# ScalarE makes the normalised nodes of a four-layer graph network's first and last layer, one activation per unit

## What is computed

```python
h = jnp.maximum(_layernorm(x, axis=-1), 0.0)
x = x + _L0_gnn_ref(h, adj, W, b)      # norm = (degree + 1e-6)^-0.5
                                       # elu(adj @ (h @ W * norm) * norm + b)
h = jnp.maximum(_layernorm(x, axis=-1), 0.0)
x = x + _L1_gnn_ref(h, adj, att_w, att_b)   # hyperbolic attention, log and exp maps
h = jnp.maximum(_layernorm(x, axis=-1), 0.0)
x = x + _L2_gnn_ref(h, adj, ...)       # message of every edge: layernorm, gelu; weighted sum
h = jnp.maximum(_layernorm(x, axis=-1), 0.0)
x = x + _L3_gnn_ref(h, adj, ...)       # four dense layers over row- and column-normed adj, tanh
```

## Time and profile before

| | us |
|---|---|
| median of three runs | 4520.15 (4515.0 to 4526.37) |
| the profiled execution, device time | 4512.91 |
| its span, first to last instruction | 4511.1 |
| mean granted TensorE clock | 0.911 of full speed |

### The profile page before, as it was taken

One profiled execution on the slowest core, in us unless ns is written; L12 is line 12 of the kernel. 1 busy time (PEld: TensorE's weight loads), 2 busy tenths in 40 slices (PEclk: granted clock), 3 DMA queues, 4 the chain that ended last, 5 costly groups with the idle time before them and its releaser, 6 DMA issues.

```text
span 4511.1 us, 101660 instructions
## 1 busy us (share of the span) xinstructions
PE 3669.4 (81%) x30593; PEld 3151.2 (70%) x31028; DVE 3454.1 (77%) x12581; ACT 2807.4 (62%) x6445; POOL 2195.7 (49%) x2282
## 2 busy tenths in 40 slices
PE   3484988879888788888878888788878878888898
PEld 2373867768677677767768677676867767676787
DVE  4788987879778687877868778786887868787750
ACT  3474856748566584765748576574856748485553
POOL 1282925528264371835628173471826528183540
PEclk7695999989899899998999899999999999999999
DMA  2000000010000101000010000001000010000000
GB/s 73 24 1 24 0 10 29 1 39 0 13 27 1 39 0 31 8 10 29 1 39 1 19 20 10 29 1 39 0 16 23 1 39 0 10 14 1 15 1 19
DMA packets 95516, 74.04 MB, mean 16 GB/s; under 512 B 7504, under 2 KB 95184, under 8 KB 95184
## 3 DMA queue, kind: packets, MB, share of 16 engines
q1 hardware_dynamic: 95184, 70.09, 5.1%
HBM read 61.68 MB, written 8.39 MB: 16 GB/s over the span
## 4 chain that ended last, share of the span: by engine, by line
PE 38%; DVE 25%; ACT 17%; issue 13%; DVEq 2%; ACTq 1%; POOL 1%; DMA 0%; SPq 0%; POOLq 0%
DVE v_z L1071 6%; PE n_bank_c L1551 6%; PE n_bank_d L1565 5%; PE n_bank_d L1568 5%; PE n_bank_d L1569 4%; PE n_bank_b L1454 4%; DVE v_pstats L1079 4%; ACT v_diag L739 4%; PE n_bank_c L1454 3%; DVE v_onehot L1061 2%; ACT v_msg L734 2%; ACT v_rows L776 1%; PE n_bank_a L1666 1%; PE n_bank_d L1465 1%; DVE v_normed L1113 1%
## 5 line engine op out<-in xcount | busy, mean ns | idle before, releaser
L516 POOL TENSOR_TENSOR v_z<-v_z,all_bc_L_gnn_be 128x512 f32<-128x512 f32 x620 | 814.3, 1314 | 86.4 <-DVE v_z L1071 86.4
L532 POOL TENSOR_TENSOR v_prstd<-v_pvar,all_neg_half 128x4 f32<-128x4 f32 x620 | 665.8, 1074 | 132.1 <-DVE v_pvar L1088 127.6
L1465 PE MATMUL n_bank_d<-v_diag,v_msg 128*128 128x128 f32 x4960 | 618.3, 278 | 24.6 <-ACT v_diag L739 24.6
L1454 PEld LDWEIGHTS n_bank_b<-v_parts,v_onehot 128*128 128x128 bf16 x8208 | 495.3, 101 | 145.4 <-ACT n_bank_b L680 101.1
L1465 PEld LDWEIGHTS n_bank_d<-v_diag,v_msg 128*128 128x128 f32 x4960 | 576.9, 192 | 27.6 <-ACT v_diag L739 27.6
L1454 PE MATMUL n_bank_b<-v_parts,v_onehot 128*128 128x128 bf16 x8208 | 535.0, 224 | 70.5 <-ACT n_bank_b L680 62.6
L739 ACT ACTIVATE v_diag<-all_ident,v_value 128x128 f32<-128x128 f32 x1860 | 572.7, 387 | 0.0
L1454 PEld LDWEIGHTS n_bank_c<-v_parts,v_onehot 128*128 128x128 bf16 x7440 | 444.2, 100 | 149.2 <-ACT n_bank_c L680 109.4
L1454 PE MATMUL n_bank_c<-v_parts,v_onehot 128*128 128x128 bf16 x7440 | 479.7, 222 | 84.2 <-ACT n_bank_c L680 81.4
L1551 PE MATMUL n_bank_c<-all_l_wsd,v_fT 128*128 128x256 f32 x1792 | 453.7, 395 | 29.4 <-ACT v_adjT L665 26.1
L675 ACT ACTIVATE v_fT<-n_bank_d,all_l_c 128x256 f32<-128x256 f32 x256 | 121.4, 475 | 530.1 <-PE n_bank_d L1569 530.1
(11 more groups left out here) (280 smaller groups left out, 7569.8 us busy)
## 6 DMA issues: line engine op xcount, KB each, us to landing
v_adj_l<-in_adj SPq DMA_DIRECT2D x128, 256.0 KB, 3.6
v_adj_x<-in_adj SPq DMA_DIRECT2D x64, 256.0 KB, 3.6
v_ring<-in_x SPq DMA_DIRECT2D x16, 512.0 KB, 5.4
out_x<-v_xout SPq DMA_DIRECT2D x64, 128.0 KB, 1.8
w_wu<-in_L_gnn_wu SPq DMA_DIRECT2D x4, 192.0 KB, 2.6
all_W<-in_L_gnn_W SPq DMA_DIRECT2D x2, 128.0 KB, 4.4
w_raw<-in_L_gnn_ws SPq DMA_DIRECT2D x1, 192.0 KB, 3.0
w_raw<-in_L_gnn_wd SPq DMA_DIRECT2D x1, 192.0 KB, 3.2
```

Source lines behind the costliest of these rows:

```text
L516: nc.gpsimd.tensor_tensor(z[par][:, units], z[par][:, units], wide(bc["L2_gnn_be1"])[:, units], ALU.add).then_inc(sem["z_ready"], 1)
L532: nc.gpsimd.tensor_tensor(prstd[:, units], pvar[:, units], minus_half[:, units], ALU.pow).then_inc(sem["prstd_ready"], 1)
L1454: ins = nc.tensor.matmul(ps_m[par][:, u], onehot[:, par, k, u * P:(u + 1) * P], parts[:, b * NB + k, t], start=False, stop=False, skip_gro ...
L1465: ins = nc.tensor.matmul(ps_agg[:, u // NB, (u % NB) * P:(u % NB + 1) * P], msg[par][:, u], diag[par][:, u], start=False, stop=False, skip ...
```

## The change

VectorE no longer makes the two sets of nodes. It makes, for all eight units at once, a scale and a bias per node (128x8 each), and ScalarE makes the nodes in one activation per unit, relu(scale * x + bias). For layer 0 the scale is rstd * norm and the bias is -mean * rstd * norm (norm is positive, so it may go inside the relu); for layer 3 they are rstd3 and -mean * rstd3. On VectorE layer0_scales stands where layer0_scaled stood, layer0_normed goes, and last_bias stands where last_features stood. On ScalarE layer0_nodes stands behind the table load L840 and before the first copy of layer 0's turned adjacency, last_nodes behind the eight Exp and before keep_sd(2). There are two new semaphores, scale0_ready and bias3_ready; hn_ready and h3_ready now come from ScalarE. In the prologue layer0_nodes(0) stands between the sign counts and the copies of the turned adjacency.

```diff
+            def layer0_nodes(z_):
+                act.wait_ge(sem["scale0_ready"], z_ + 1)
+                act.sem_inc(keep["held"], 1)
+                first = act.snap((z_ % RING) * GB)
+                xg = ring[:, bass.ds(first, GB)].rearrange("p b k d -> p (b k) d")
+                for u in range(UNITS):
+                    ins = nc.scalar.activation(hn[:, u], xg[:, u], ACT.Relu, bias=bias0[:, u:u + 1], scale=scale0[:, u:u + 1])
+                    if u % NB == NB - 1:
+                        ins.then_inc(sem["hn_ready"], 1)
+
+            def last_nodes(g):
+                act.wait_ge(sem["bias3_ready"], g + 1)
+                act.sem_inc(keep["held"], 1)
+                first = act.snap((g % RING) * GB)
+                xg = ring[:, bass.ds(first, GB)].rearrange("p b k d -> p (b k) d")
+                flat = h3[:].rearrange("p b k d -> p (b k) d")
+                for u in range(UNITS):
+                    ins = nc.scalar.activation(flat[:, u], xg[:, u], ACT.Relu, bias=bias3[:, u:u + 1], scale=rstd3[:, u:u + 1])
+                ins.then_inc(sem["h3_ready"], 1)
...
                     act.preload_act_table_set(EXP_TABLES)
+                if l0:
+                    layer0_nodes(z_)
+                if l1:
                     if l0:
                         act.wait_ge(sem["gated"], a * GB + GB)
...
                         nc.scalar.activation(total[:, b], total[:, b], ACT.Exp, scale=-0.5).then_inc(sem["coef_ready"], 1)
+                if u:
+                    last_nodes(g)
                 if l3:
                     keep_sd(t, 2, 0)
...
                 count_signs(0, u)
+            layer0_nodes(0)
             for b in range(GB):
                 layer0_keep_adjT(0, b)
...
-            def layer0_normed(z_):
+            def layer0_scales(z_):
                 dve.wait_ge(sem["rstd0_ready"], z_ + 1)
-                xg = nodes(z_)
-                for u in range(UNITS):
-                    v.tensor_scalar(normed[:, u], xg[:, u], mv0[:, u, 0:1], rstd[:, u:u + 1], ALU.subtract, ALU.mult)
+                dve.wait_ge(sem["norm_ready"], z_ + 1)
+                v.tensor_tensor(scale0[:], rstd[:], norm[:], ALU.mult)
                 dve.drain()
-
-            def layer0_scaled(z_):
-                dve.wait_ge(sem["norm_ready"], z_ + 1)
-                for b in range(GB):
-                    for u in range(b * NB, (b + 1) * NB):
-                        ins = v.tensor_scalar(hn[:, u], normed[:, u], 0.0, norm[:, u:u + 1], ALU.max, ALU.mult)
-                    ins.then_inc(sem["hn_ready"], 1)
+                v.scalar_tensor_tensor(bias0[:], mv0[:, :, 0], -1.0, scale0[:], ALU.mult, ALU.mult)\
+                    .then_inc(sem["scale0_ready"], 1)
...
-                def last_features():
-                    xg = nodes(g)
-                    flat = h3[:].rearrange("p b k d -> p (b k) d")
+                def last_bias():
                     dve.wait_ge(sem["rstd3_ready"], g + 1)
-                    for i in range(UNITS):
-                        v.tensor_scalar(flat[:, i], xg[:, i], mv3[:, i, 0:1], rstd3[:, i:i + 1], ALU.subtract, ALU.mult)
-                    dve.drain()
-                    v.tensor_scalar(flat, flat, 0.0, None, ALU.max)\
-                        .then_inc(sem["h3_ready"], 1)
+                    v.scalar_tensor_tensor(bias3[:], mv3[:, :, 0], -1.0, rstd3[:], ALU.mult, ALU.mult)\
+                        .then_inc(sem["bias3_ready"], 1)
```

More of the change, by code:

```diff
@@ L313, in network @@
         var = plan.sb("var", [P, UNITS])
+        scale0 = plan.sb("scale0", [P, UNITS])
+        bias0 = plan.sb("bias0", [P, UNITS])
+        bias3 = plan.sb("bias3", [P, UNITS])
         rstd = plan.sb("rstd", [P, UNITS])
@@ L346, in network @@
         names = ("consts", "w1_ready",
-                 "degree_ready", "eps_ready", "norm_ready", "var0_ready", "rstd0_ready", "hn_ready", "adj_turned",
+                 "degree_ready", "eps_ready", "norm_ready", "var0_ready", "rstd0_ready", "scale0_ready", "hn_ready", "adj_turned",
                  "adjT_kept", "sum_made", "sum_kept", "out_made", "z0_low_ready", "exp_ready", "x0_ready", "var1_ready",
@@ L360, in network @@
                  "upd_made", "upd_read", "upd_var_ready", "upd_rstd_ready", "upd_scaled", "upd_shifted", "x2_ready",
-                 "mv3_ready", "var3_ready", "rstd3_ready", "h3_ready", "h3_turned", "h3_kept", "adj3_turned",
+                 "mv3_ready", "var3_ready", "rstd3_ready", "bias3_ready", "h3_ready", "h3_turned", "h3_kept", "adj3_turned",
                  "adjT3_kept", "row_squared", "col_squared", "summed3", "clamped3", "inv_ready", "norms_spread",
@@ L1331, in mix @@
                     update_normed()
-                if l0:
-                    layer0_normed(z_)
                 if l3:
@@ L1353, in mix @@
                 if l0:
-                    layer0_scaled(z_)
+                    layer0_scales(z_)
                 if l1:
@@ L1360, in mix @@
                 if u:
-                    last_features()
+                    last_bias()
                 if l1:
@@ L1384, in mix @@
                     pick(first_ahead + 1, 1)
-            for piece in (layer0_stats, layer0_eps, layer0_normed, layer0_scaled, layer0_z, layer0_finish):
+            for piece in (layer0_stats, layer0_eps, layer0_scales, layer0_z, layer0_finish):
                 piece(0)
```

## The result

The changed kernel takes 4601.2 us (median of 4 runs, 4597.0 to 4604.2) against 4521.3 of the kernel before on the same chip: ratio 1.0177, 95% interval 1.0159 to 1.0194, 80 us slower. The forecast was 4588, 68 us slower. The profiled execution of after took 4599.5 us (span 4597.7), 86.6 us more span than that of before.

A forecast was written before the change was run, and what follows sets the result against it. No engine bounds the whole: the chain is 38% TensorE, 25% VectorE, 17% ScalarE. Blocks 48.6, clock 16.9, mix(14) 4.7, start 3.1 and early passes -5.7 sum to 67.6 us more: 4588 us, range 4552 to 4614.

The forecast's parts named there:

- Relu price, first block: layer0_nodes before L640: 0.38 us per Relu, 3.05 us per block, all delaying TensorE's third turn.
- The clock: Behind TensorE's longer gap before the third turn: low clock costs 1.69 us in ten more passes, 16.9 us.
- Second block: last_nodes between the Exp and L671: 2.1 us of 3.05 covered, so 1.0 us per looped pass.
- mix(2): VectorE's path was 4.0 us behind the other there; ScalarE's comes 4.05 later, L1654 starts unchanged: 0.
- Early passes: mix(-1) and mix(0), where VectorE is the path: its saved work gives -5.7 us together.
- Start and mix(14): Before the first mix TensorE waits 3.1 us more; mix(14)'s uncovered second block plus clock costs 4.7 us.
- VectorE's wait before the coefficients: Before L1228 in the looped passes: VectorE's wait was to become 12 to 13 us, from 4.41 in mix(11).
- the clock stays up: Rival: TensorE's clock does not fall behind the longer gap; 4569 us, chance 0.10.
- a cheaper Relu: Rival: a Relu on ScalarE costs no more than L739; 4567 us, chance 0.10.
- a table load: Rival: each Relu block brings its own 1.28 us table load, or ring addresses delay ScalarE; 4622 us, chance 0.06.
- hidden blocks: Rival: both Relu blocks fall into ScalarE's own waits for TensorE; 4517 us, chance 0.05.
- VectorE late: Rival: VectorE is late in the looped passes, so its saved 2.7 us count 13 times; 4479 us, chance 0.03.

The follow-up runs named there:

- extra_8: Kernel before, plus eight unread 128x128 Relus on ScalarE where the change puts layer 0's block; 4589.3 us, ratio 1.0159.
- moved_l0: Changed kernel with layer 0's eight Relus moved between ScalarE's second and third Tanh of the last layer's first level; 4545.4 us, ratio 1.0055.
- fill_12: Changed kernel plus twelve fp32 matmuls with unread results on TensorE in the gap before the third turn; 4575.6 us, ratio 1.0138 to the kernel before.
- extra_4: Kernel before, plus four unread 128x128 Relus on ScalarE where the change puts layer 0's block; 4557.2 us, ratio 1.0096.
- l3_only: Changed kernel with layer 0's nodes back on VectorE, only the last layer's nodes on ScalarE; 4541.7 us, ratio 1.0049.
- late_ln: Changed kernel with both Relu blocks in ScalarE's waits and the four Ln moved behind the second level's last Tanh; 4472.2 us, ratio 0.9909.

## Why the prediction was right, and where its terms were off

- **Relu price, first block.** Forecast 0.38 us each and 3.05 a block, all of it on the path; 0.386 and 3.09 measured, and the wait grew from 2.61 to 5.68, by 3.07, in every looped pass. extra_8 shows that delay alone does it, moved_l0 that the place decides. By the figures of the Trainium skill, "ScalarE: Activation LUTs", section "What ACT_TABLE_LOAD costs" (186 ns and 0.833 ns a column, 93 ns more for each pointer operand, neighbours overlapping by 93 ns), such a Relu would come every 387 ns, an estimate. The trace agrees with its 0.386 us.
- **The clock: right mechanism, term too small.** Forecast 16.9 us (1.69 in ten passes); the mean rose by 8.08 - 5.89 = 2.19 us, 28.5 us in 13 passes. I took the price from mix(4), whose gap is 2.61 us and whose granted clock from the turn to the third level is 0.76; behind the longer gap it is 0.67 there, so the bound of 2.6 us was the value. fill_12 shows that the low clock is the gap's. extra_4 shows that a gap of 4.14 us costs what mix(4) paid, 1.6 us, but in nearly every pass; only behind 5.68 us is it more.
- **Second block.** Forecast 1.0 us with 2.1 covered; 1.11 in twelve passes (34.74 against 33.63), with the new wait of 0.94 us before L1563. Alone, in l3_only, the block costs 1.9 us a pass; the 1.2 us behind the support go with a lower clock there (0.81 against 0.84), and why it is lower is open.
- **mix(2).** Forecast 0: it went from 164.5 to 165.2 us. TensorE's wait before the support went from 8.71 to 4.69 us, as in the other passes: VectorE's selection no longer ends last there, as forecast.
- **Early passes.** Forecast -5.7, measured -7.6. The two terms taken at L969's place were near by luck. L969 takes 1.65 us in mix(11) but 4.72 in mix(-1), while GpSimd makes its sums, and what replaces it is slow there as well:

```profile
121.03 4.72 DVE L969 TENSOR_SCALAR v_hn<-v_normed,v_norm 128x128 f32<-128x128 f32 x8
...
120.96 3.72 POOL L580 TENSOR_TENSOR v_total<-v_pair 128x512 f32<-128x512 f32 x3 [0.36 <-ACT v_pair L839]
```

These are of the kernel before. In mix(-1) of after:

```profile
123.31 1.23 DVE L990 TENSOR_TENSOR v_scale<-v_rstd,v_norm 128x8 f32<-128x8 f32 x1
124.62 1.15 DVE L992 SCALAR_TENSOR_TENSOR v_bias<-v_mv,v_scale 128x8 f32<-128x8 f32 x1
126.47 0.69 DVE L1224 TENSOR_SCALAR v_pair<-n_bank_b 128x512 f32<-128x512 f32 x1 [0.70 <-PE n_bank_b L1656]
```

From the place to the start of clamp_pair(3) pass 4.64 us before and 3.16 after: 1.5 less, the forecast's number from other lengths. The other 1.8 us of the 3.3 were in no term: 0.3 ahead of the place, 0.6 behind it up to the support, 0.9 from there to the gathers. In mix(0) the sum was right (-4.3 against -4.2) with its parts -1.1 and -3.1, not -1.6 and -2.6.

- **Start and mix(14).** Forecast 3.1 and 4.7, measured 2.5 and 3.5. The wait before L1563 in mix(14) is 4.48 us, 4.45 was said.
- **VectorE's wait before the coefficients** was to be 12 to 13 us. It is 9.95 in mix(11), with another 4.46 before L1000, where VectorE now waits for TensorE's products of layer 0: the time saved does turn into waiting, but at two places.
- **Not foreseen:** 10.0 us in slots and behind mix(14). No run shows that the change brings them. 4.6 of them are slots(6), which took 109.6 us in the profiled run of before and 114.0 to 115.1 in every other trace; extra_8 has such a short one in slots(9). Another 2.8 lie behind mix(14), from its gathers to the end: 290.4 to 291.8 us in before and four other kernels, 294.4 to 294.9 in the rest, among them extra_8, in which VectorE makes all the nodes. What decides is open.
- **The sum.** 86.6 in the trace against 67.6: the clock +11.6, the rest of the looped passes +1.1, the slots and the end +10.0, start, mix(14) and early passes -3.7. In the medians the difference is 80, since the profiled run of before lay 8 us under its median and that of after 2. That the 68 us of the forecast come within 12 of these 80 is in part luck: in the traces the forecast missed 19 us, and the two profiled runs' distances from their medians hide 7 of them. The rivals fell: the clock stays up (fill_12 shows what that would look like), a cheaper Relu, a table load, hidden blocks, and VectorE late, which became true only in late_ln's order.

## What to carry to other kernels

Before moving work to an engine with time to spare, find in its timeline what is queued behind the place and who waits for that; ScalarE was idle for 530 us before its Tanh alone, and the same sixteen Relus cost 80 us in front of two awaited copies and nothing inside those waits. A wait on TensorE's path is to be priced twice, once for its length and once for the low clock behind it, and the second price comes from a row with a gap of that length. And a change that frees an engine off the path can still be worth its time after the order is mended: try the order first, then the change again.

## What the chip showed that was not expected

- What the low clock behind a gap on TensorE costs grew with the gap in steps and only up to a point: 1.7 us in three of 13 passes and nothing in ten behind 2.61 us, 1.6 in eleven behind 4.14, 2.6 on average behind both 5.68 and 8.77.
- Matmuls with a useless result in the gap (24 instructions, 5.2 us) kept the granted clock at 1.00 and made the changed kernel about 18 us faster.
- A small VectorE instruction can take many times its usual time: layer0_scales' product of 128x8 took 0.16 us in mix(11) of after and 1.23 us in mix(-1) (shown above), there while GpSimd made its sums. That GpSimd is the cause fits both traces and was not tested.

```profile
3364.31 0.16 DVE L990 TENSOR_TENSOR v_scale<-v_rstd,v_norm 128x8 f32<-128x8 f32 x1
```
